# Trace layer of a four-layer kernel: earlier context scan, fuller column tiles, output with tokens on the partitions

## The chip, the cores and the metric

The kernel runs on one core of a Trainium2 chip. The metric is the device time of one execution in microseconds (us). TensorE is PE in the profile, VectorE is DVE, ScalarE is ACT, GpSimd is POOL, SyncE is SP.

## What is computed

`x` is 32 batches of 256 tokens by 256 channels. Four layers run one after the other, each with a residual: sparse attention, a trace layer, an expert MLP, a last attention. The change touches the second one alone:

```python
ctx = causal_ema(x, tau_ctx)                                  # h[t] = alpha*h[t-1] + x[t]
wg = sigmoid(concat([x, ctx]) @ Wg.T + bg)
gated = x * wg
h1 = gelu(x @ Wn1.T + bn1)
mod = 0.5 + sigmoid(h1 @ Wn2.T + bn2)                         # 32 traces per token
traces = [causal_ema(gated * mod[..., d], tau_raws[d]) for d in range(32)]
temporal = sum_d traces[d] * softmax(blend)[d]
gate = sigmoid(temporal @ Wtemp.T + btemp)
soma = gelu(x @ Wsoma.T + bsoma)
out = (soma * gate) @ Wout.T
out = (out - out.mean(-1)) / sqrt(out.var(-1) + 1e-5) * gamma + beta
x = x + out
```

## The kernel before

All 32 batches of `x` stay in SBUF (`X`), with the channels on the partitions (2 blocks of 128) and the 256 tokens in the free dimension. A layer is one block of five hand-written instruction streams, one for each engine, with semaphores between them; nothing reorders them. In the trace layer (`trace_layer`) every engine goes through the same loop over the batches: `body(0)`, then 15 times two bodies, then `body(31)`. The body of batch n mixes three batches: the inputs and gates of batch n + 1 (`has_a`), the traces of batch n, and the output of batch n - 1 (`has_c`).

**Split products.** A product of two fp32 matrices is made of three fp32r matmuls on high and low parts (`product`, L1267). A high part is an ACT copy to fp32r; a low part is a subtraction, made by POOL for `x` and the context (`low_inputs`, L907 and L909) and by DVE for `temporal` and `mixed` (L1038 and L1042).

**Context.** DVE scans the two channel blocks of the next batch (`context`, L938) at the start of a body; ACT makes the high part, POOL the low part, and PE uses both in `gate_in`.

**Traces.** The tokens are cut into chunks of 8. What reaches a chunk from earlier ones: PE sums gated inputs against decay factors (`states`, L1317; POOL prepares the factors in `decays`, L897), DVE weighs the sums by the blend (`state`, L1011), and PE spreads them over the tokens of a chunk (`spread`, L1328). A spread matmul is 128 rows by 32 columns of the array; its output lands on 32 partitions of `pY`, chosen by `tile_position=(0, 32*j)`. There are four calls of `spread` in a batch, of two matmuls each, with j = 0, 1 or 2, 3. ACT copies the result out (`outer_t`, L1174), PE turns it back to channels (`turn_back`, L1336). Inside a chunk, eight lags are made by PE (`lags`, L1345) into two PSUM buffers and summed by DVE (`lag_sum`, L1020 to L1028). DVE's `total` (L1034) adds both parts to `temporal`.

**Output of batch n - 1.** ACT makes the high part of `temporal` (L1133), DVE the low part (L1038), PE the product with Wtemp (`gate_out`, into `pY`), ACT the tanh (L1187), DVE `mixed` (L1048) and its low part, PE the product with Wout (`output`, channels on the partitions of `pZ`). The mean is already taken out of Wout. For the variance ACT squares `pZ` (L1193), PE multiplies the squares by a matrix of 1/256 (`mean_square`, L1372, plain fp32), which leaves the same variance on all partitions; ACT takes the root (L1198) and then calls a Gelu on one column to have that table loaded again (L1200); DVE takes the reciprocal of 128x256 (L1054) and multiplies (L1057); ACT applies gamma and beta (`scaling`, L1206), POOL adds the result to `X` (`residual`, L903).

**Around a batch's end** PE runs states 3, spread 2, lags 6, spread 3, lags 7, `soma_in` (the product with Wsoma), `turn` (transposes of the gated input of batch n + 1), `turn_back`, lags 0 and 1 and states 0 and 1 of batch n + 1, and then `gate_out(n)`, which begins with this wait:

```python
        def gate_out(n):
            pe.wait_ge(templo_done, n + 1)
```

Of the kernel before, what the change touches and what calls it, by code (L numbers as in the profile page):

```python
# [14 lines left out]
P = 128  # L15
S = 256
# [725 lines left out]
def trace_layer(nc, sem_ctx, ctx, t, X, NB, consts):  # L742
# [17 lines left out]
    def sem(name):  # L760
# [36 lines left out]
    mean_mat = sb("mean_mat", [P, P])  # L797
# [14 lines left out]
    state = [sb(f"state{i}", [P, 2, D]) for i in range(2)]  # L812
# [7 lines left out]
    square = sb("square", [P, C, S])  # L820
    std = sb("std", [P, S])
    rstd = sb("rstd", [P, S])
    normed = sb("normed", [P, C, S])
    scaled = sb("scaled", [P, C, S])
# [19 lines left out]
    out_mm, sq_done, var_mm, std_done, rstd_done, normed_done, scaled_done, x2_done = (  # L844
        sem(n) for n in ("out_mm", "sq", "var_mm", "std", "rstd", "normed", "scaled", "x2"))
# [16 lines left out]
    def loop(eng, body):  # L862

        body(0, 0, True, False)
        if NB > 2:
            with pairs(eng, 1, NB - 1) as n:
                body(n, 1, True, True)
                body(n + 1, 0, True, True)
        body(NB - 1, 1, False, True)
# [13 lines left out]
    def _(pool):  # L883
# [27 lines left out]
        def body(n, par, has_a, has_c):  # L911
# [6 lines left out]
        low_inputs(0, 0)  # L918
        pool.wait_ge(set_done, 1)
        decays(0, 0)  # L920
        loop(pool, body)
# [4 lines left out]
    def _(dve):  # L926
# [16 lines left out]
        link(dve.memset(mean_mat[:], 1.0 / D))  # L943
# [107 lines left out]
        def norm(n):  # L1051
# [3 lines left out]
            dve.wait_ge(rstd_done, n + 1)  # L1055
            at_least(dve, scaled_done, n)
            dve.tensor_tensor(normed[:], pZ[:], rstd[:].unsqueeze(1).to_broadcast([P, C, S]), ALU.mult).then_inc(normed_done, 1)  # L1057

        def body(n, par, has_a, has_c):
            if has_a:  # L1060
# [883 lines left out]
```

## Time and profile before

| | us |
|---|---|
| median of 3 runs (2218.88 to 2220.06) | 2219.59 |
| span of the profiled execution | 2220.5 |
| PE busy | 2051.3 (92% of the span) |
| DVE busy | 1699.0 (77%) |
| ACT busy | 1196.2 (54%) |
| POOL busy | 796.4 (36%) |

The profiled execution comes with its span and with no device time of its own; the span stands 0.9 us above the median of the runs. The second layer takes from about 950 to 1703 us of the span; the chain that ended last goes back only into the fourth layer, since a barrier stands between layers, so this chain tells nothing of the second. Busy times of PE are those of pipelined matmuls and overlap: a matmul that lasts 0.28 us can be followed by the next after 0.12 us. Start-to-start distances are the better measure of what a stretch of PE costs.

### The profile page before, as it was taken

How to read it: one execution, taken by the hardware profiler on the slowest of the kernel's cores; microseconds unless marked ns; L12 is line 12 of the kernel's file. 1: busy time of each engine (PE TensorE's matmuls, PEld its weight loads, DVE VectorE, ACT ScalarE, POOL GpSimd, SP SyncE). 2: the span in 40 equal slices, each digit the busy share in tenths (PEclk: the TensorE clock that was granted, in tenths of full speed). 3: DMA queues.
4: the chain of work that ended last, by engine and by line, in shares of the span. 5: the costliest groups of instructions: out<-in, count | busy, mean ns of one | idle time of the engine just before them, and what ended most of it. 6: DMA issues, size and time to landing. Idle time of an engine off the chain costs nothing. (4 is left out here: it accounts for less than half of the span.)

```text
span 2220.5 us, 42789 instructions
## 1 busy us (share of the span) xinstructions
PE 2051.3 (92%) x14158; PEld 1652.1 (74%) x14158; DVE 1699.0 (77%) x2530; ACT 1196.2 (54%) x2428; POOL 796.4 (36%) x589
## 2 busy tenths in 40 slices
PE   3899999999999999759999999999995999999998
PEld 2566666666666666447777777777774999999997
DVE  6788888888888888577878888887875566666664
ACT  2466565666665666435555555555554555555553
POOL 4645444444455554033333333333340111111111
PEclk8999999999999999879999999999997999999998
DMA  3444444444444444100000000000001222222221
GB/s 92 106 106 107 107 110 110 108 109 108 105 105 106 108 109 104 24 25 1 0 0 0 0 0 0 0 0 0 0 0 59 78 79 70 85 69 80 85 66 60
DMA packets 121171, 137.47 MB, mean 62 GB/s; under 512 B 24240, under 2 KB 89776, under 8 KB 121136
## 3 DMA queue, kind: packets, MB, share of 16 engines
q1 hardware_dynamic: 118576, 128.64, 22.9%
q0 software_dynamic: 2560, 8.39, 1.0%
q8 instruction: 19, 0.31, 0.1%
q14 instruction: 16, 0.13, 0.0%
HBM read 48.35 MB, written 8.39 MB: 26 GB/s over the span
## 5 line engine op out<-in xcount | busy, mean ns | idle before, releaser
L366 DVE TENSOR_REDUCE a_neg_max<-a_s 128x2 f32<-128x512 f32 x512 | 329.1, 683 | 123.4 <-PE a_s L613 121.8
L487 ACT ACTIVATE a_e<-a_t 128x512 f32<-128x512 f32 x512 | 281.2, 610 | 228.4 <-PE a_t L626 228.4
L375 DVE SCALAR_TENSOR_TENSOR a_e<-a_e,a_w_t 128x1024 f32<-128x1024 f32 x256 | 373.6, 1469 | 4.1 <-ACT a_e L487 4.1
L613 PE MATMUL a_s<-a_k_st,a_q_st 96*128 96x256 f32 x1024 | 275.4, 380 | 0.0
L613 PEld LDWEIGHTS a_s<-a_k_st,a_q_st 96*128 96x128 f32 x1024 | 203.5, 199 | 13.7
L610 PE MATMUL a_s<-a_add_m,ident_bf 128*128 128x512 bf16 x512 | 201.8, 394 | 7.9 <-POOL a_add_m L254 5.8
L1695 ACT ACTIVATE c_hid<-c_pH,c_b 128x256 f32<-128x256 f32 x256 | 107.4, 471 | 186.3 <-PE c_pH L1758 185.9
L897 POOL TENSOR_TENSOR b_decayed<-b_table,b_mod_t 128x1024 f32<-128x1024 f32 x64 | 118.6, 1872 | 210.3 <-ACT b_mod_t L1163 203.0
L1317 PE MATMUL b_pS<-b_gated_t,b_decayed 128*128 128x256 f32 x768 | 189.5, 390 | 0.7
L626 PE MATMUL a_t<-a_q_st,a_k_st 97*128 97x512 f32 x512 | 177.1, 426 | 2.6 <-DMA a_q_st<-a_max_row 2.0
L642 PE MATMUL a_v<-a_e,a_v_pad 128*32 128x256 f32 x2048 | 163.6, 392 | 4.5 <-DVE a_e L375 2.1
L1317 PEld LDWEIGHTS b_pS<-b_gated_t,b_decayed 128*128 128x128 f32 x768 | 139.3, 191 | 35.1 <-issue 19.7
L1758 PE MATMUL c_pH<-c_x_hi,c_w_hi 128*128 128x256 f32 x512 | 149.8, 293 | 15.4 <-DVE c_w_lo L1660 15.2
L281 POOL TENSOR_TENSOR x_all<-a_delta,x_all 128x512 f32 (+1 forms) x32 | 46.6, 1456 | 323.1 <-ACT a_delta L468 323.1
L1573 POOL TENSOR_TENSOR c_w2b_lo<-c_we,c_w2b_hi 128x512 fp32r<-128x512 f32 x32 | 54.9, 1714 | 277.5 <-ACT c_w2b_hi L1688 277.5
L1758 PE MATMUL c_pH<-c_x_hi,c_w_lo 128*128 128x256 f32 x512 | 145.5, 284 | 0.0
L1758 PE MATMUL c_pH<-c_x_lo,c_w_hi 128*128 128x256 f32 x512 | 145.0, 283 | 0.0
L1028 DVE TENSOR_TENSOR b_inner<-b_inner,b_prod 128x448 f32<-128x448 f32 (+6 forms) x224 | 122.5, 547 | 23.8
L1599 DVE CAST c_hid_hi<-c_hid 128x512 fp32r<-128x512 f32 x128 | 54.5, 425 | 111.2 <-PE c_pO L1772 91.8
L610 PEld LDWEIGHTS a_s<-a_add_m,ident_bf 128*128 128x128 bf16 x512 | 49.6, 97 | 116.3 <-issue 69.8
L1011 DVE TENSOR_TENSOR b_state<-b_pS,b_w_rep 128x512 f32<-128x512 f32 x128 | 85.2, 685 | 56.3 <-PE b_pS L1317 56.3
L1345 PE MATMUL b_pL<-b_mod_st,b_w_st 96*128 96x256 f32 x512 | 116.1, 319 | 2.3 <-DVE b_mod_st L1005 1.0
(261 smaller groups left out, 5720.4 us busy)
## 6 DMA issues: line engine op xcount, KB each, us to landing
a_q_st<-a_q_hi SPq DMA_DIRECT2D x256, 128.0 KB, 2.4
a_k_st<-a_k_hi SPq DMA_DIRECT2D x256, 64.0 KB, 2.0
a_q_st<-a_q_lo SPq DMA_DIRECT2D x128, 128.0 KB, 2.4
a_xs<-in_xT SPq DMA_DIRECT2D x32, 256.0 KB, 2.8
a_k_st<-a_k_lo SPq DMA_DIRECT2D x128, 64.0 KB, 2.1
x_all<-in_xT SPq DMA_DIRECT2D x32, 256.0 KB, 2.8
c_we<-in_we SPq DMA_DIRECT2D x32, 256.0 KB, 2.7
c_key_t<-in_keyT SPq DMA_DIRECT2D x32, 256.0 KB, 3.2
```

Source lines behind the costliest of these rows:

```text
L366: dve.tensor_reduce(neg_max[:, qc, head:head + 2], ps_s[b][:], AX.X, ALU.max, negate=True).then_inc(red_done, 1)
L375: dve.scalar_tensor_tensor(out=buf[:], in0=buf[:], scalar=BIG, in1=w_t[par][:, kc].unsqueeze(1).to_broadcast([P, 4, S]), op0=ALU.min, op1= ...
L487: act.activation(e[g % E_BUFS][:, 2 * b:2 * b + 2], ps_t[b][:], ACT.Exp).then_inc(exp_done, 1)
L610: pe.matmul(ps_s[b][:], ident_bf[:], add_m[par][:, qc].unsqueeze(1).to_broadcast([P, 2, S]), start=True, stop=False)
L613: ins = pe.matmul(ps_s[b][:, r], q_st[par][0:96, slot, qc * P:qc * P + P], k_st[par][0:96, slot // 2], start=False, stop=(r == 1))
L626: pe.matmul(ps_t[b][:], k_st[par][0:97, pair, kc * P:kc * P + P], q_st[par][0:97, 2 * pair:2 * pair + 2], start=True, stop=True).then_inc( ...
L642: ins = pe.matmul(ps_v[half][32 * j:32 * j + 32, quad // 2], v_pad[par][:, kc, 4 * quad + j], e[g % E_BUFS][:, j], start=(g % 4 == 0), sto ...
L897: ins = pool.tensor_tensor(decayed[par][:, lo:lo + cnt], table[:, lo:lo + cnt], mod_t[:, k].unsqueeze(1).to_broadcast([P, cnt, TRACES]), A ...
L1028: dve.tensor_tensor(y, y, pr, ALU.add).then_inc(inner_done, 1)
L1317: ins = pe.matmul(pS[q % 2][:, i], decayed[par][:, lo:lo + 4].rearrange("p a d -> p (a d)"), gated_t[par][:, k], start=(k == 0), stop=(k = ...
L1345: ins = pe.matmul(pL[lag % 2][:, c], w_st[0:3 * TRACES, lag, c * P:c * P + P], mod_st[par][:], start=True, stop=True)
L1758: ins = pe.matmul(pH[r][:, i], w[:, k, m * P:m * P + P], x[par][:, k], start=(w is w1_hi and x is x_hi and k == 0), stop=(x is x_lo and k ...
```

## The change

Bodies of the loop now exist in the forms first, second, 14 times two, last but one, last, since the context runs two batches ahead.

- **Context.** `context(n + 2)` runs in the middle of body n on DVE (after `modulation`), `context(1)` before the loop. DVE's `lag_sum(n, 0)` comes before `low_temporal(n - 1)`, and each other lag sum moves up by one place. ACT's `high_context(n + 2)` stands after `scaling(n - 1)`, ahead of `turned`. POOL's `low_context(n + 2)` is the last of its body, behind `residual(n - 1)`.
- **Spread.** Four `state` buffers in place of two; `spread(n, h)` is called twice with four matmuls, j = 0 to 3, and waits for the second state of its half.
- **Output.** `product(pZ[:, m], mixed_p, wout_p, ...)`: the operands are exchanged, so that tokens lie on the partitions. ACT's `deviation` squares each block of 128x256 with `accum_out` into one column, takes the root of 128x2; DVE's `norm` is a reciprocal of 128x2; ACT's `normalized` multiplies by it. PE turns the result back (`turn_normed`, four transposes into `pB`, after lags 7), and ACT's `scaling` reads `pB`. The matmul with 1/256, and DVE's multiplication, are gone.

```diff
-        def low_inputs(n, par):
+        def low_x(n, par):
             pool.wait_ge(xhi_done, n + 1)
...
+        def low_context(n):
             pool.wait_ge(chi_done, n + 1)
...
         def body(n, par, has_a, has_c, has_x):
             if has_a:
-                low_inputs(n + 1, 1 - par)
+                low_x(n + 1, 1 - par)
+            if has_a:
                 decays(n + 1, 1 - par)
             if has_c:
                 residual(n - 1)
+            if has_x:
+                low_context(n + 2)
...
+        def deviation(n):
             act.wait_ge(out_mm, n + 1)
+            for m in range(C):
+                act.activation(square[:], pZ[:, m], ACT.Square, accum_out=var[:, m:m + 1]).then_inc(sq_done, 1)
+                act.wait_ge(sq_done, C * n + m + 1)
             at_least(act, rstd_done, n)
-            act.activation(std[:], pB[:, 0], ACT.Sqrt, bias=eps[:]).then_inc(std_done, 1)
+            act.activation(std[:], var[:], ACT.Sqrt, bias=eps[:], scale=1.0 / D).then_inc(std_done, 1)
...
+        def normalized(n):
+            act.wait_ge(rstd_done, n + 1)
+            at_least(act, back_done, n)
+            for m in range(C):
+                ins = act.activation(normed[:, m], pZ[:, m], ACT.Copy, scale=rstd[:, m:m + 1])
+            ins.then_inc(normed_done, 1)
...
+        def spread(n, h):
+
+            pe.wait_ge(sw_done, 4 * n + 2 * h + 2)
...
+            for j in range(4):
+                ins = pe.matmul(pY[32 * j:32 * j + 32, h], spread_w[:], state[2 * h + j // 2][:, j % 2],
                                 start=True, stop=True, tile_position=(0, 32 * j))
...
+        def turn_normed(n):
...
+            pe.wait_ge(normed_done, n + 1)
+            for m in range(C):
+                for c in range(C):
+                    ins = pe.transpose(pB[:, c, m * P:m * P + P], normed[:, m, c * P:c * P + P], ident[:])
+            ins.then_inc(back_done, 1)
```

Two places show how the instructions move. The first is PE in a loop body, from states 3 to `soma_in` (`b_pS` is states, `b_pL` lags, `b_spread_w` the spread). Before:

```order
L1317 MATMUL b_pS<-b_gated_t,b_decayed 128x256 x4
L1323 REGISTER_ALU
L1328 MATMUL b_pY<-b_state,b_spread_w 32x256 x2
L1343 REGISTER_ALU
L1345 MATMUL b_pL<-b_mod_st,b_w_st 128x256 x2
L1323 REGISTER_ALU
L1328 MATMUL b_pY<-b_state,b_spread_w 32x256 x2
L1343 REGISTER_ALU
L1345 MATMUL b_pL<-b_mod_st,b_w_st 128x256 x2
L1267 MATMUL b_pZ<-b_x_hi,b_wsoma_hi 128x256
```

After:

```order
L1329 MATMUL b_pS<-b_gated_t,b_decayed 128x256 x4
L1354 REGISTER_ALU
L1356 MATMUL b_pL<-b_mod_st,b_w_st 128x256 x2
L1335 REGISTER_ALU
L1339 MATMUL b_pY<-b_state,b_spread_w 32x256 x4
L1354 REGISTER_ALU
L1356 MATMUL b_pL<-b_mod_st,b_w_st 128x256 x2
L1384 MATMUL b_pB<-ident,b_wtemp 128x128 x4
L1279 MATMUL b_pZ<-b_x_hi,b_wsoma_hi 128x256
```

Of two spreads with two matmuls, one with four is left, lags 6 comes before it, and the transposes of `normed` (which now shares the storage of `b_wtemp`) stand between lags 7 and `soma_in`.

The second place is the end of a body and the start of the next. POOL before (`b_decayed` is `decays`, `x_all<-b_scaled` the residual):

```order
L897 TENSOR_TENSOR b_decayed<-b_table,b_mod_t 128x512
L903 ISA
L903 TENSOR_TENSOR x_all<-b_scaled,x_all 128x2x256
L906 REGISTER_ALU
L907 ISA
L907 TENSOR_TENSOR b_x_lo<-x_all,b_x_hi 128x512
L909 TENSOR_TENSOR b_ctx_lo<-b_ctx_e,b_ctx_hi 128x512
```

POOL after (`b_wtemp` and `b_wsoma` are now also the storage of `normed` and `scaled`):

```order
L898 TENSOR_TENSOR b_decayed<-b_table,b_mod_t 128x512
L904 ISA
L904 TENSOR_TENSOR x_all<-b_wsoma,x_all 128x2x256
L911 REGISTER_ALU
L912 TENSOR_TENSOR b_ctx_lo<-b_ctx_e,b_ctx_hi 128x512
L908 ISA
L908 TENSOR_TENSOR b_x_lo<-x_all,b_x_hi 128x512
```

The context's low part has moved from behind the low part of `x` to between it and the residual.

DVE at the same place, before:

```order
L1034 TENSOR_TENSOR b_temporal<-b_inner,b_pY 128x512
L938 ISA
L938 SCALAR_TENSOR_TENSOR b_ctx_e<-b_alpha_c,x_all 128x256
L938 ISA
L938 SCALAR_TENSOR_TENSOR b_ctx_e<-b_alpha_c,x_all 128x256
L1038 TENSOR_TENSOR b_temp_lo<-b_temporal,b_temp_hi 128x512
L1008 ISA
L1010 REGISTER_ALU
L1011 TENSOR_TENSOR b_state<-b_pS,b_w_rep 128x512
```

DVE after:

```order
L1042 TENSOR_TENSOR b_temporal<-b_inner,b_pY 128x512
L1023 ISA
L1028 TENSOR_TENSOR b_inner<-b_gated,b_pL 128x512
L1046 TENSOR_TENSOR b_temp_lo<-b_temporal,b_temp_hi 128x512
L1016 ISA
L1018 REGISTER_ALU
L1019 TENSOR_TENSOR b_state<-b_pS,b_w_rep 128x512
L1016 REGISTER_ALU
L1019 TENSOR_TENSOR b_state<-b_pS,b_w_rep 128x512
```

The two scans between `total` and the low part of `temporal` are gone from here, and the first lag product has taken their place.

## Rows read from the trace of the kernel before

**Rows 1.** Stages, second layer (window: us, busy PE PEld DVE ACT POOL, PEclk, DMA)
```profile
1000.00:1600.00 600.00, 565.98 (x3779) 469.61 (x3780) 485.69 (x836) 321.82 (x620) 226.85 (x135) 1.00 0.00 0
```

**Rows 2.** Timeline of PE, one batch: start, duration, line, tiles, count [idle before]
```profile
1200.54 0.39 PE L1267 MATMUL b_pY<-b_temp_hi,b_wtemp_hi 128*128 128x256 f32 x1 [1.23 <-DVE b_temp_lo L1038]
...
1207.75 0.63 PE L1328 MATMUL b_pY<-b_state,b_spread_w 128*32 128x256 f32 x4
1208.31 1.99 PE L1317 MATMUL b_pS<-b_gated_t,b_decayed 128*128 128x256 f32 x8
1210.14 1.03 PE L1372 MATMUL b_pB<-b_square,b_mean_mat 128*128 128x256 f32 x4
1210.82 0.59 PE L1345 MATMUL b_pL<-b_mod_st,b_w_st 96*128 96x256 f32 x2
...
1214.74 0.62 PE L1328 MATMUL b_pY<-b_state,b_spread_w 128*32 128x256 f32 x4
...
1215.72 0.63 PE L1328 MATMUL b_pY<-b_state,b_spread_w 128*32 128x256 f32 x4
...
1216.62 0.28 PE L1267 MATMUL b_pZ<-b_x_hi,b_wsoma_hi 128*128 128x256 f32 x1
...
1218.05 0.60 PE L1302 MATMUL b_pA<-ident,b_gated 128*128 128x128 f32 x4
1218.49 0.60 PE L1336 MATMUL b_pY<-ident,b_outer_t 128*128 128x128 f32 x4
...
1219.52 1.99 PE L1317 MATMUL b_pS<-b_gated_t,b_decayed 128*128 128x256 f32 x8
1222.84 0.39 PE L1267 MATMUL b_pY<-b_temp_hi,b_wtemp_hi 128*128 128x256 f32 x1 [1.33 <-DVE b_temp_lo L1038]
```

**Rows 3.** Timeline of DVE, the same batch
```profile
1214.84 0.69 DVE L1011 TENSOR_TENSOR b_state<-b_pS,b_w_rep 128x512 f32<-128x512 f32 x1
...
1217.20 0.98 DVE L1028 TENSOR_TENSOR b_inner<-b_inner,b_prod 128x128 f32<-128x128 f32 x1
...
1219.29 0.69 DVE L1034 TENSOR_TENSOR b_temporal<-b_inner,b_pY 128x512 f32<-128x512 f32 x1 [0.52 <-PE b_pY L1336]
1219.91 2.30 DVE L938 TENSOR_TENSOR_SCAN b_ctx_e<-b_alpha_c,x_all 128x256 f32<-128x256 f32 x2
1222.13 0.66 DVE L1038 TENSOR_TENSOR b_temp_lo<-b_temporal,b_temp_hi 128x512 fp32r<-128x512 f32 x1
```

**Rows 4.** Timeline of PE in the first layer: four column tiles at once
```profile
405.32 0.64 PE L642 MATMUL a_v<-a_e,a_v_pad 128*32 128x256 f32 x8
```

**Rows 5.** Timeline of POOL, the same batch
```profile
1216.22 1.81 POOL L903 TENSOR_TENSOR x_all<-b_scaled,x_all 128x512 f32 x1 [3.98 <-ACT b_scaled L1206]
1220.03 1.63 POOL L907 TENSOR_TENSOR b_x_lo<-x_all,b_x_hi 128x512 fp32r<-128x512 f32 x1 [2.00 <-ACT b_x_hi L1123]
1223.03 1.31 POOL L909 TENSOR_TENSOR b_ctx_lo<-b_ctx_e,b_ctx_hi 128x512 fp32r<-128x512 f32 x1 [1.37 <-ACT b_ctx_hi L1128]
```

**Rows 6.** Timeline of ACT, the same batch
```profile
1211.20 0.48 ACT L1198 ACTIVATE b_std<-b_pB,b_eps 128x256 f32<-128x256 f32 x1 [1.05 <-PE b_pB L1372]
...
1213.10 0.82 ACT L1144 ACTIVATE b_th_g<-b_pA,b_bg 128x256 f32<-128x256 f32 x2
1214.94 1.09 ACT L1206 ACTIVATE b_scaled<-b_normed,b_beta,b_gamma 128x256 f32<-128x256 f32 x2 [1.02 <-DVE b_normed L1057]
...
1218.69 0.60 ACT L1169 ACTIVATE b_gated_t<-b_pA 128x512 f32<-128x512 f32 x1 [1.69 <-PE b_pA L1302]
...
1220.01 0.63 ACT L1133 ACTIVATE b_temp_hi<-b_temporal 128x512 fp32r<-128x512 f32 x1 [0.18 <-DVE b_temporal L1034]
```

**Rows 7.** Groups of instructions by line, fourth layer, ACT (count | busy us, mean ns)
```profile
L1703 ACT ACTIVATION_READ_ACCUMULATOR c_prob<-c_pS,c_neg_max 128x1 f32 x62 | 12.2, 196 | 0.0
```

**Rows 8.** Busy time by stage, last body of the second layer (columns as in rows 1)
```profile
1668.00:1672.50 4.50, 2.68 (x17) 1.62 (x16) 3.61 (x7) 1.47 (x3) 0.00 (x0) 1.00 0.00 0
1673.00:1675.50 2.50, 2.50 (x14) 1.89 (x12) 1.26 (x3) 0.47 (x1) 0.00 (x0) 0.50 0.01 3
```

More of the change, by code:

```diff
@@ L811, in trace_layer @@
     decayed = [sb(f"decayed{i}", [P, TABLE, TRACES]) for i in range(2)]
-    state = [sb(f"state{i}", [P, 2, D]) for i in range(2)]
+    state = [sb(f"state{i}", [P, 2, D]) for i in range(4)]
     inner = sb("inner", [P, C, S])
@@ L819, in trace_layer @@
     mixed = sb("mixed", [P, C, S])
[L820 to L824, printed above, removed]
+    square = sb("square", [P, D])
+    var = sb("var", [P, C])
+    std = sb("std", [P, C])
+    rstd = sb("rstd", [P, C])
+    normed = wtemp
+    scaled = wsoma
     pA = ps("pA", [P, C, S])
@@ L862, in loop @@
     def loop(eng, body):
[L864 to L869, printed above, removed]
+        body(0, 0, True, False, True)
+        body(1, 1, True, True, True)
+        with pairs(eng, 2, NB - 2) as n:
+            body(n, 0, True, True, True)
+            body(n + 1, 1, True, True, True)
+        body(NB - 2, 0, True, True, False)
+        body(NB - 1, 1, False, True, False)
     @block.sync
@@ L1054, in norm, with body @@
             dve.reciprocal(rstd[:], std[:]).then_inc(rstd_done, 1)
[L1055 to L1060, printed above, removed]
-                context(n + 1)
+        def body(n, par, has_a, has_c, has_x):
+            lag_sum(n, par, 0)
             if has_c:
@@ L1086, in body @@
             total(n)
+        context(1)
         gating(0, 0)
@@ L1231, in body @@
             if has_c:
+                normalized(n - 1)
+            spread_out(n)
+            if has_c:
                 scaling(n - 1)
-            spread_out(n)
+            if has_x:
+                high_context(n + 2)
             if has_a:
@@ L1248, in _ @@
         high_mixed(NB - 1)
[L1249 removed]
         deviation(NB - 1)
+        normalized(NB - 1)
         scaling(NB - 1)
@@ L1319, in states @@
             ins.then_inc(st_done, 1)
-        def spread(n, q):
-            pe.wait_ge(sw_done, 4 * n + q + 1)
-            if q == 0:
+        def spread(n, h):
+            pe.wait_ge(sw_done, 4 * n + 2 * h + 2)
+            if h == 0:
                 at_least(pe, tho_done, n)
-            for i in range(2):
-                j = (2 * q + i) % 4
-                ins = pe.matmul(pY[32 * j:32 * j + 32, q // 2], spread_w[:], state[q % 2][:, i],
+            for j in range(4):
+                ins = pe.matmul(pY[32 * j:32 * j + 32, h], spread_w[:], state[2 * h + j // 2][:, j % 2],
                                 start=True, stop=True, tile_position=(0, 32 * j))
@@ L1363, in output, with body @@
             for m in range(C):
-                ins = product(pZ[:, m], wout_p, mixed_p, [(k, k) for k in range(C)], m)
+                ins = product(pZ[:, m], mixed_p, wout_p, [(k, k) for k in range(C)], m)
             ins.then_inc(out_mm, 1)
-        def mean_square(n):
+        def turn_normed(n):
             pe.wait_ge(tht_done, NB if isinstance(n, int) and n + 3 > NB else n + 3)
-            pe.wait_ge(sq_done, n + 1)
-            for k in range(C):
-                ins = pe.matmul(pB[:, 0], mean_mat[:], square[:, k], start=(k == 0), stop=(k == C - 1))
-            ins.then_inc(var_mm, 1)
-        def body(n, par, has_a, has_c):
+            pe.wait_ge(normed_done, n + 1)
[3 more added lines that the diff above has]
+            ins.then_inc(back_done, 1)
+        def body(n, par, has_a, has_c, has_x):
             lags(n, par, 0)
@@ L1390, in body @@
                 modulate_rows(n + 1)
+            spread(n, 0)
             if has_c:
```

62 lines of the change are left out of this document (26 added, 36 removed).

## Prediction

> **What bounds the kernel now.** The layers are separated by barriers, so I read the second layer's own stages first and the chain that ended last not at all: it ends in the fourth layer. In 600 us of steady second layer PE is busy for 566 us, DVE for 486, ACT for 322, POOL for 227, and PE's granted clock is 1.00, its upper level of 2.4 GHz [rows 1]. So PE is the bound, nearly full, and a batch can only become shorter by less PE work or less PE waiting.
>
> Then PE's timeline of one batch. `gate_out` starts at 1200.54 and again at 1222.84, so the period is 22.30 us [rows 2]. PE has one real wait in it: the states that start at 1219.52 need 1.83 us (1208.31 to 1210.14 for the same eight records), so PE is free at 1221.35 and starts `gate_out` at 1222.84. That wait is 1.49 us [rows 2].
>
> Then DVE, to see why. `total` starts at 1219.29, ACT has the high part of `temporal` ready at 1220.01 + 0.63 = 1220.64, but DVE stands in two scans from 1219.91 and makes the low part only at 1222.13 [rows 3, 6].
>
> Last, who slows whom. The residual on POOL takes 1.81 us and its neighbour of the same 128x512 takes 1.31 [rows 5]. A DVE sum of 128x128 which reads SBUF twice takes 0.98 us, and it ends at 1218.18, just after the residual's end at 1218.03 [rows 3, 5]. POOL's low part of x runs from 1220.03 to 1221.66, and the second scan ends at 1222.21, 0.55 us after it [rows 3, 5]. So an operation of DVE with two SBUF inputs and a POOL operation do not run beside each other: the later one waits for the whole of the earlier one, and then DVE needs 0.55 us more.
>
> **The change part by part, on PE.** I compare one period with 22.30.
>
> *Scans moved.* The wait of 1.49 us goes, as far as the low part of `temporal` comes in time (below). In mid-batch DVE has room: it loses the big reciprocal and the multiplication, and was busy 486 of 600 us.
>
> *Spreads.* A spread of two matmuls costs 0.56 us (1207.75 to 1208.31) [rows 2]. Four matmuls of the same 128x32 by 256 on four column tiles last 0.64 us in the first layer, where two last 0.63 here [rows 2, 4]: four cost what two do. The bounds are 0.56 and 1.12 us for four; I take 0.56, since that row is the same shape. The first half saves 0.56. The second saves less. Before, spread 3 started 0.98 us after spread 2 (1214.74 to 1215.72) [rows 2], with lags 6 in between and state 3 ready meanwhile. Now the only spread follows lags 6 and must wait for state 3, whose weighing starts 0.10 us after states 3 and lasts 0.69 [rows 3]: about 0.83 us with the handoff. Gain 0.15, and PE has a new wait of some 0.4 us there; lags 7 and everything of the batch's end stand behind it.
>
> *Variance.* The matmul with 1/256 goes: 0.68 us (1210.14 to 1210.82) [rows 2]. Four transposes come: 0.44 us as `turn` (1218.05 to 1218.49), at most the 0.68 that it replaces [rows 2]; I take 0.60 for the change of kind of matmul behind it. The exchange of operands in `output` changes neither count nor shape: nothing. `gate_out` to `output` stays as long as before, since the chain over tanh, `mixed` and its low part crosses a lag sum on DVE as before, only the next smaller one.
>
> Sum on PE, if the low part is in time: 22.30 - 1.49 - 0.56 - 0.15 - 0.68 + 0.60 = 20.02 us.
>
> **The batch's end after the change.** Let T be the start of the new transposes. `soma_in` takes 1.43 us (1216.62 to 1218.05) [rows 2], so `turn` starts at T + 2.03, PE is free for `gate_out` 0.44 + 1.03 + 1.83 = 3.30 later (1218.05, 1218.49, 1219.52 [rows 2]), at T + 5.33. DVE's `total` starts 1.24 us after `turn`, ACT's high part 0.72 after that [rows 2, 3, 6], and it ends 0.63 later: the low part can start at T + 4.65 (a lag product of 0.6 us fits in front of it). It takes 0.66 and ends at T + 5.31: just in time.
>
> Now POOL. Transposes to their reader on ACT: 0.64 us (1218.05 to 1218.69) [rows 2, 6]. `scaling` from PSUM: 0.82 as the two tanh [rows 6]; handoff to POOL 0.19 (1214.94 + 1.09 to 1216.22) [rows 5, 6]. The residual starts at T + 1.65 and takes 1.31, as nothing of DVE with two SBUF inputs runs then; the context's low part, whose input ACT has made by then, takes 1.31 more, to T + 4.27. The low part of x for the next batch follows at once (before the change it started 1.98 us after `turn`, 1218.05 to 1220.03 [rows 2, 5], so its input is there by T + 4.0) and holds POOL from T + 4.3 to T + 5.6. DVE's low part of `temporal` arrives at T + 4.65, 0.35 us too late. It then ends at T + 5.6 + 0.55 = T + 6.15, and `gate_out` starts 0.05 later (1222.13 + 0.66 to 1222.84 [rows 2, 3]) at T + 6.2 in place of T + 5.33. Price: 0.84 us a batch, so the period is 20.86 and the gain 1.44 us.
>
> The Trainium skill (SBUF — State Buffer, "SBUF: two separate sides") says the same: a DVE operation with two SBUF inputs and a GpSimd operation that reads SBUF share a port pair, and whichever starts first "gets the pair for the whole instruction; the other fully blocks". This rule speaks against the change, which puts three POOL operations in a row right where DVE's critical subtraction falls; without it the sum would be the 20.02 above. The trace agrees, with the 0.98 and the 1.81 us named above.
>
> **Outside the steady batches.** Thirty periods get the full gain. Ahead of the loop DVE now runs two scans (2.3 us) before `gated(0)`, and body 0 loses them: about nothing. At the end the three DVE and PE steps of the last norm give way to steps on ACT and transposes: between -2 and +2. The sum: 30 x 1.44 = 43 us. The profiled span is 0.9 us above the median, so I subtract from the median: 2219.6 - 43 = **2176 us**.
>
> **Rivals.**
>
> A, the forecast: the low part of x gets ahead of the low part of `temporal`. For it: 0.35 us of lead. Chance 0.56, own range 2166 to 2186.
>
> B: the lead is not there. Handoffs in a row on POOL of 0.1 us more each, or transposes of 0.44, would turn the order. Then DVE's subtraction runs first, POOL waits where nobody needs it, and the period is 20.0 to 20.1: 30 x 2.25 = 67 us, 2152 us. Chance 0.30.
>
> C: the new transposes wait for their input, or four tiles don't overlap. ACT's chain is longer by two read-outs of the accumulator (0.20 each [rows 7]) and by cutting one square in two, and shorter by the 1.05 us that the root waited for PE [rows 6]; so the gate's tanh starts some 0.6 us earlier than its 12.56 us after `gate_out` (1213.10), and the normalized blocks (2 x 0.82 later) are there about 13.6 us after `gate_out`, where PE comes at 14.7 (`turn` came at 17.51 before, 0.79 less after the sum above, and T lies 2.03 ahead of it). The slack is 1.1 us. If ACT is 1.9 us later than this, 0.8 us a batch is lost: 2176 + 24 = 2200 us. Spreads that cost 1.12 give 1.1 us back a batch, 2209 us, which the row of the first layer speaks against. Chance 0.09 together.
>
> D, slower than before: the clock. In the last body, with PE busy 2.68 of 4.50 us, the granted clock is 1.00 and then 0.50 (1.2 GHz) in the following stretch of full work [rows 8]. The steady loop now has two waits, 0.4 and 0.84 us, in place of one of 1.49. If they brought such a fall in each batch, work of 1.44 us at half the speed takes as much again: from there on the gain is gone, and with 2 us of work the kernel is slower by 30 x 0.56 = 17 us, 2236 us. Against it: the loop took its 1.49 us at a granted clock of 1.00 [rows 1], and the new waits are 6 us apart and smaller together. Chance 0.03. That nothing comes of it at all, the gain lost in one place and the rest in another, has 0.02.
>
> **Numbers.** Forecast 2176. From 2149 (B with a batch 0.1 us shorter) to 2188, below C's times; about 0.1 lies above, the rest of B below. A measurement of this kernel tells a change of about 0.2% (4.4 us) from none. A, B and C are all faster: 0.95. Within 0.2%: 0.02. Slower: 0.03.
>
> **What would show it.** In the changed profile: `gate_out` to `gate_out` 20.9 us; a wait of about 0.4 us before the second spread, released by the state; spreads of eight records at 0.56 to 0.65 us; the low part of `temporal` lasting 1.4 us or more in place of 0.66 and ending 0.55 us after POOL's low part of x; a wait of 0.8 us before `gate_out`. A `gate_out` that follows the states at once, and a low part of 0.66 us, would be B. A wait ahead of the transposes released by ACT would be C, a granted clock under 1.00 in the loop D.

## The result and the profile after

| | before | changed |
|---|---|---|
| median, us | 2219.82 (2218.88 to 2220.47) | 2169.43 (2167.51 to 2170.3) |
| span of the profiled execution, us | 2220.5 | 2167.9 |
| a batch of the steady second layer, us | 22.29 | 20.64 |

The ratio is 0.9772, with a 95% interval of 0.9758 to 0.9786. The change makes the kernel faster by 50 us, or 2.3%. The forecast was 2176 us with a range of 2149 to 2188, by case A.

The steady second layer of the changed kernel, in the stretch and columns of [rows 1]:

```profile
1000.00:1600.00 600.00, 559.35 (x4075) 485.49 (x4074) 454.40 (x873) 368.70 (x815) 223.81 (x145) 1.00 0.00 0
```

PE is busy for 559 of 600 us, 7 less than before, since it now waits in two places. DVE lost 31 us and ACT gained 47. The granted clock is 1.00 as before. More batches fit: 4075 matmul records against 3779.

PE's timeline of one batch of the changed kernel, which answers to [rows 2]:

```profile
1203.86 0.39 PE L1279 MATMUL b_pY<-b_temp_hi,b_wtemp_hi 128*128 128x256 f32 x1 [0.80 <-DVE b_temp_lo L1046]
...
1208.52 0.64 PE L1339 MATMUL b_pY<-b_state,b_spread_w 128*32 128x256 f32 x8
1209.09 0.39 PE L1279 MATMUL b_pZ<-b_wout_hi,b_mixed_hi 128*128 128x256 f32 x1
...
1210.99 1.97 PE L1329 MATMUL b_pS<-b_gated_t,b_decayed 128*128 128x256 f32 x8
1212.61 0.58 PE L1356 MATMUL b_pL<-b_mod_st,b_w_st 96*128 96x256 f32 x2
...
1214.71 1.89 PE L1329 MATMUL b_pS<-b_gated_t,b_decayed 128*128 128x256 f32 x8
1216.25 0.58 PE L1356 MATMUL b_pL<-b_mod_st,b_w_st 96*128 96x256 f32 x2
1217.38 0.64 PE L1339 MATMUL b_pY<-b_state,b_spread_w 128*32 128x256 f32 x8 [0.56 <-DVE b_state L1019]
1217.95 0.50 PE L1356 MATMUL b_pL<-b_mod_st,b_w_st 96*128 96x256 f32 x2
1218.29 0.60 PE L1384 MATMUL b_pB<-ident,b_wtemp 128*128 128x128 f32 x4
1218.65 0.36 PE L1279 MATMUL b_pZ<-b_x_hi,b_wsoma_hi 128*128 128x256 f32 x1
...
1220.16 0.60 PE L1314 MATMUL b_pA<-ident,b_gated 128*128 128x128 f32 x4
...
1221.71 1.99 PE L1329 MATMUL b_pS<-b_gated_t,b_decayed 128*128 128x256 f32 x8
1224.50 0.39 PE L1279 MATMUL b_pY<-b_temp_hi,b_wtemp_hi 128*128 128x256 f32 x1 [0.80 <-DVE b_temp_lo L1046]
```

`gate_out` to `gate_out` is 20.64 us in this batch. The prediction's T is 1218.29. Both spreads are of eight records and last 0.57 us from start to start of what follows. The two waits stand where the prediction put them: the profile lists 0.56 us ahead of the second spread, for the state, and 0.80 ahead of `gate_out`, for the low part of `temporal`. A listed wait is shorter than one taken from start to start, as the prediction takes them, since it begins where the profile lets the last matmul end: the prediction's 1.49 us before the change is listed as 1.33 [rows 2].

What DVE and POOL did at the batch's end, in answer to [rows 3] and [rows 5], DVE first:

```profile
1210.92 1.27 DVE L946 TENSOR_TENSOR_SCAN b_ctx_e<-b_alpha_c,x_all 128x256 f32<-128x256 f32 x2
...
1216.64 0.69 DVE L1019 TENSOR_TENSOR b_state<-b_pS,b_w_rep 128x512 f32<-128x512 f32 x1 [0.57 <-PE b_pS L1329]
...
1222.18 0.69 DVE L1028 TENSOR_TENSOR b_inner<-b_gated,b_pL 128x512 f32<-128x512 f32 x1
1222.85 1.59 DVE L1046 TENSOR_TENSOR b_temp_lo<-b_temporal,b_temp_hi 128x512 fp32r<-128x512 f32 x1
```

Then POOL:

```profile
1220.14 1.28 POOL L904 TENSOR_TENSOR x_all<-b_wsoma,x_all 128x512 f32 x1 [4.34 <-ACT b_wsoma L1217]
1221.37 1.29 POOL L912 TENSOR_TENSOR b_ctx_lo<-b_ctx_e,b_ctx_hi 128x512 fp32r<-128x512 f32 x1
1222.63 1.26 POOL L908 TENSOR_TENSOR b_x_lo<-x_all,b_x_hi 128x512 fp32r<-128x512 f32 x1
```

The low part of x starts 0.22 us before the low part of `temporal` and ends at 1223.89. DVE's subtraction, begun at 1222.85, ends at 1224.44: 0.55 us after POOL's end, and 1.59 us long where it was 0.66. The two scans, now in mid-batch, take 1.27 us together where they took 2.30.

The scaling no longer starts after a root that waited for PE; it starts behind the new transposes (ACT's timeline, in answer to [rows 6]):

```profile
1218.93 1.02 ACT L1217 ACTIVATE b_wsoma<-b_pB,b_beta,b_gamma 128x256 f32<-128x256 f32 x2 [0.25 <-PE b_pB L1384]
...
1222.19 0.63 ACT L1139 ACTIVATE b_temp_hi<-b_temporal 128x512 fp32r<-128x512 f32 x1 [0.17 <-DVE b_temporal L1042]
```

### The profile page after: what moved, and what is told of

Same layout as the page of the kernel before. It is cut to its first block and busy times, and to the rows that moved or that the text cites. A ratio compares the mean times of both kernels' runs of the same rounds, so it can differ in the third digit from the quotient of the medians.

```text
span 2167.9 us, 42832 instructions
## 1 busy us (share of the span) xinstructions
PE 1993.4 (92%) x14158; PEld 1630.0 (75%) x14158; DVE 1620.8 (75%) x2498; ACT 1220.5 (56%) x2588; POOL 776.8 (36%) x589
## 3 DMA queue, kind: packets, MB, share of 16 engines
q1 hardware_dynamic: 118576, 128.64, 23.1%
## 5 line engine op out<-in xcount | busy, mean ns | idle before, releaser
L898 POOL TENSOR_TENSOR b_decayed<-b_table,b_mod_t 128x1024 f32<-128x1024 f32 x64 | 127.1, 2007 | 270.6 <-ACT b_mod_t L1169 263.3
L1329 PEld LDWEIGHTS b_pS<-b_gated_t,b_decayed 128*128 128x128 f32 x768 | 139.6, 191 | 22.3 <-issue 6.7
L1036 DVE TENSOR_TENSOR b_inner<-b_inner,b_prod 128x448 f32<-128x448 f32 (+6 forms) x224 | 113.2, 505 | 22.7
L1031 DVE TENSOR_TENSOR b_prod<-b_gated,b_pL 128x448 f32<-128x448 f32 (+6 forms) x224 | 94.2, 421 | 36.5 <-PE b_pL L1356 36.4
L440 ACT ACTIVATE a_q_full<-a_bank,a_bq_s,par_mask 128x256 f32<-128x256 f32 x128 | 65.8, 574 | 89.7 <-PE a_bank L575 75.4
```

What stands on the lines that cost most here:

```text
L898: ins = pool.tensor_tensor(decayed[par][:, lo:lo + cnt], table[:, lo:lo + cnt], mod_t[:, k].unsqueeze(1).to_broadcast([P, cnt, TRACES]), A ...
L1036: dve.tensor_tensor(y, y, pr, ALU.add).then_inc(inner_done, 1)
L1329: ins = pe.matmul(pS[q % 2][:, i], decayed[par][:, lo:lo + 4].rearrange("p a d -> p (a d)"), gated_t[par][:, k], start=(k == 0), stop=(k = ...
```

## The experiments

Every ratio below is against the kernel before, timed beside the kernel in question. The theory under test is case A with the sum behind it; the rivals are that other parts carry the gain. "Period" is the time from one batch's high part of `temporal` to the next, for odd and even batches where they differ.

### Is it POOL that holds the low part?

The first kernel puts POOL's low part of x behind DVE's low part of `temporal`.

```diff
             if has_a:
+                at_least(pool, templo_done, n)
                 low_x(n + 1, 1 - par)
```

> The changed kernel, in which POOL's low part of x waits until DVE has made the low part of temporal. Theory (the two operations exclude each other and POOL is ahead by 0.22 us): DVE's low part takes 0.66 to 0.69 us in place of 1.6, the wait before gate_out goes, the period falls from 20.69 by 0.8 us to about 19.9, the time from 2169 to about 2145. Rival (gate_out is late for another reason, such as ACT's high part or the lag product ahead of it): the low part is not shorter or the wait stays, and the time is 2169 or a little more, since the wait puts POOL's work later.

Measured: 2144.28 us, ratio 0.9658 (0.9641 to 0.9674), period 19.77 and 19.83. Timeline of this kernel, DVE and then POOL:

```profile
1212.90 0.69 DVE L1047 TENSOR_TENSOR b_temp_lo<-b_temporal,b_temp_hi 128x512 fp32r<-128x512 f32 x1
```

```profile
1213.86 1.29 POOL L908 TENSOR_TENSOR b_x_lo<-x_all,b_x_hi 128x512 fp32r<-128x512 f32 x1 [1.17 <-DVE b_temp_lo L1047]
```

The low part takes 0.69 us again, and PE's wait ahead of `gate_out` is gone from its list of waits (23.3 us in 29 times in the changed kernel, between 1000 and 1600 us). The period falls by 0.84 us, which is the price that the prediction gave. It shows the price, but a wait on a semaphore also orders more than the two operations. So the next two leave all waits as they are and only shift POOL, by small memsets behind the context's low part. They write storage that nobody reads.

```diff
+    idle = sb("idle", [P, 16])
...
             if has_x:
                 low_context(n + 2)
+                for i in range(4):
+                    pool.memset(idle[:, 4 * i:4 * i + 4], 0.0)
```

> The changed kernel with four idle memsets of 128x4 on POOL between the context's low part and the low part of x; no wait is added. Theory (whoever starts first has the port for its whole operation, and POOL leads by 0.22 us): if the four together take more than 0.22 us the order turns over, DVE's low part takes 0.66 to 0.69 us, and the time is about 2145 us although POOL has more to do. Rival (the two share bandwidth, or DVE's low part is slow by itself): it stays near 1.6 us or ends later by the length of the memsets, and the time is 2169 to 2180 us.

Measured: 2172.59 us, ratio 0.9785 (0.9769 to 0.9802), period 20.68 and 20.86. The order did not turn over. POOL and DVE of this kernel:

```profile
1222.59 0.19 POOL L925 MEMSET b_idle<- 128x4 f32 x4
1222.75 1.26 POOL L909 TENSOR_TENSOR b_x_lo<-x_all,b_x_hi 128x512 fp32r<-128x512 f32 x1
```

```profile
1222.86 1.70 DVE L1049 TENSOR_TENSOR b_temp_lo<-b_temporal,b_temp_hi 128x512 fp32r<-128x512 f32 x1
```

The four memsets took only 0.2 us. POOL's lead of 0.22 us shrank to 0.11, and DVE's subtraction became longer by the 0.11, since it still ends 0.55 after POOL. The batch became 0.13 us longer by it (20.64 to 20.77 on average); the times, 2169.43 and 2172.59 us, are too near each other to tell the two kernels apart by their ratios. Twelve memsets in the same place are the test of the turn-over:

> As e2, but with twelve memsets in place of four. Four took 0.20 us together and moved POOL's low part of x by 0.12 us; its lead over DVE's low part fell from 0.22 to 0.11 us and the low part of temporal ended 0.1 us later. Twelve take about 0.6 us. Theory (first come, whole operation): POOL now comes 0.3 us late, DVE's low part takes 0.69 us, the period falls to 19.8 us and the time to about 2145 us. Rival (every delay of POOL is passed on): each further 0.1 us costs 3 us, so about 2182 us.

Measured: 2143.92 us, ratio 0.9651 (0.9635 to 0.9667), period 19.65 and 19.75.

```profile
1213.96 0.69 DVE L1049 TENSOR_TENSOR b_temp_lo<-b_temporal,b_temp_hi 128x512 fp32r<-128x512 f32 x1
```

```profile
1213.70 0.44 POOL L925 MEMSET b_idle<- 128x4 f32 x12
1214.38 1.44 POOL L909 TENSOR_TENSOR b_x_lo<-x_all,b_x_hi 128x512 fp32r<-128x512 f32 x1 [0.24 <-issue]
```

Twelve instructions of no use on POOL, 0.68 us with their issue, make the kernel 26 us faster than the change alone. No wait, no engine's order and no matmul is different from the kernel with four. The low part of x now meets an operation already running and is the one that is stretched (1.44), where nobody needs it. This is the test that A needed: which of the two operations comes first decides 0.84 us a batch by the first of these kernels and 1.07 by the last two (20.77 to 19.70, on average). The rule of the Trainium skill that the prediction cites, that whichever starts first has the shared ports for its whole instruction (SBUF — State Buffer, "SBUF: two separate sides"), agrees with both kernels with memsets: with four, DVE comes second and takes 1.70 us; with twelve, POOL does and takes 1.44.

The third way is to give POOL the low part of x first and the context's after it. The kernel before had them in that order.

```diff
             if has_a:
                 low_x(n + 1, 1 - par)
-            if has_a:
+                low_context(n + 1)
                 decays(n + 1, 1 - par)
             if has_c:
                 residual(n - 1)
-            if has_x:
-                low_context(n + 2)
...
-        low_context(1)
```

> The changed kernel with POOL's low part of x ahead of the context's low part again; nothing else moved. Theory (first come, whole operation): the low part of x starts when its high part is there, 3.85 us after the transposes of the normalized block, and holds POOL to 5.1; DVE's low part, which wants to start at 4.56, ends at 5.65 in place of 6.16. Period 20.64 to 20.15 us, time about 2154 us. Rival (any order is as good as that with the wait of e1, since POOL is done sooner): 2145 us; or no effect: 2169.

Measured: 2159.82 us (2154 expected), ratio 0.9713 (0.9696 to 0.9731), period 20.16 and 20.28. POOL and DVE of this kernel:

```profile
1220.73 1.28 POOL L908 TENSOR_TENSOR b_x_lo<-x_all,b_x_hi 128x512 fp32r<-128x512 f32 x1 [0.81 <-ACT b_x_hi L1126]
1221.96 1.75 POOL L912 TENSOR_TENSOR b_ctx_lo<-b_ctx_e,b_ctx_hi 128x512 fp32r<-128x512 f32 x1
```

```profile
1221.36 1.20 DVE L1043 TENSOR_TENSOR b_temp_lo<-b_temporal,b_temp_hi 128x512 fp32r<-128x512 f32 x1
```

The low part of `temporal` comes in the middle of the low part of x. It still ends 0.55 after it (1222.01 and 1222.56), but POOL's end lies earlier, so it takes 1.20 us and not 1.59. The context's low part, the next on POOL, was begun at 1221.96 and takes 1.75, to 1223.71: DVE, which was already waiting, went between two operations of POOL. So this order gives about half of what the other two kernels give (0.42 us of the batch).

### What each part is worth

The spread alone is undone: four spreads of two matmuls, in their old places.

```diff
-            for j in range(4):
-                ins = pe.matmul(pY[32 * j:32 * j + 32, h], spread_w[:], state[2 * h + j // 2][:, j % 2],
+            for i in range(2):
+                j = (2 * q + i) % 4
+                ins = pe.matmul(pY[32 * j:32 * j + 32, q // 2], spread_w[:], state[q][:, i],
...
             states(n, par, 3)
+            spread(n, 2)
             lags(n, par, 6)
-            spread(n, 1)
+            spread(n, 3)
```

> The changed kernel with four spreads of two matmuls again, each in its old place; context and output stay changed. Theory (PE is the bound up to each wait, four tiles cost what two do): one spread of 0.56 us more ahead of states 2, and the second spread starts 0.98 us after the matmuls of state 3 were followed by a spread, about 0.13 us later than now: 0.69 us a batch, time about 2190 us. Rival (the batch is bound by the chain over DVE and ACT, and PE's extra work only fills its waits): 2169 to 2175 us.

Measured: 2193.94 us (2190 expected), ratio 0.9877 (0.9861 to 0.9894), period 21.35 and 21.50. PE's waits between 1000 and 1600 us (us in total, times, longest) have one row left:

```profile
PE b_pY L1279 <- DVE b_temp_lo L1046: 23.3, 28, 0.9
```

The wait for the state is gone with the second spread's new place, and 0.78 us a batch is lost. The prediction's terms for the spreads were 0.56 + 0.15 = 0.71.

The context is put back to the start of a body, on DVE, ACT and POOL:

```diff
         def body(n, par, has_a, has_c, has_x):
+            if has_a:
+                context(n + 1)
             lag_sum(n, par, 0)
             if has_c:
                 low_temporal(n - 1)
...
-            if has_x:
-                context(n + 2)
             lag_sum(n, par, 4)
...
```

> The changed kernel with the context scanned at the start of the body for the next batch again (DVE, ACT and POOL in the old order there); spreads and output stay changed. Theory (scans, lag product and low part in a row on DVE, with POOL's low part of x between the two scans): the low part ends 1.15 us later than in the changed kernel, period 21.8, time about 2204 us. Rival (the lock has eaten what moving the context gave, since POOL's low context now stands in the same place): within 6 us of 2169.

Measured: 2225.0 us (2216.81 to 2226.47), ratio 1.0007 (0.9995 to 1.0018): no faster than the kernel before, and 21 us over the 2204 expected. Batches last either 21.6 to 21.8 us, as the theory has it, or 23.1 to 23.3, some 18 of 30. Here are a long batch's wait, and busy time and granted clock (the last but two columns) in four stretches, three behind that wait and one behind the next, of 1.83 us, which ended at 1223.82; last the row of the whole stretch.

```profile
1200.62 0.39 PE L1275 MATMUL b_pY<-b_temp_hi,b_wtemp_hi 128*128 128x256 f32 x1 [1.84 <-DVE b_temp_lo L1043]
```

```profile
1200.60:1203.50 2.90, 2.88 (x18) 2.88 (x19) 2.33 (x5) 1.09 (x3) 1.12 (x1) 0.74 0.00 0
1203.60:1206.50 2.90, 2.90 (x18) 2.85 (x18) 2.31 (x5) 1.03 (x2) 0.00 (x0) 0.69 0.00 0
1206.80:1209.00 2.20, 2.20 (x23) 1.78 (x22) 1.57 (x5) 0.38 (x1) 0.00 (x0) 1.00 0.00 0
1223.80:1226.00 2.20, 2.19 (x18) 2.19 (x19) 2.17 (x4) 0.62 (x3) 1.12 (x1) 1.00 0.00 0
...
1000.00:1600.00 600.00, 536.32 (x3729) 468.21 (x3728) 408.84 (x799) 340.57 (x748) 216.29 (x132) 0.95 0.00 0
```

Behind the wait of 1.84 us PE is fully busy, at a granted clock of 0.74 and then 0.69: part of the time at 1.2 GHz, and the rest at 2.4. Behind the next wait it is 1.00. So not each such wait brings the clock down, but 18 of 30 batches show it. This kernel also has the wait of 0.56 us for the state in each batch. That is the mechanism of case D, in a kernel that the prediction did not ask about. To show it as the cause, a further kernel fills the wait: the same, with twelve matmuls (Wsoma with x, into `pA`, used by nobody) ahead of `gate_out`.

```diff
             states(n, par, 1)
             if has_c:
+                for m in range(C):
+                    product(pA[:, m], wsoma_p, x_p[par], [(k, k) for k in range(C)], m)
                 gate_out(n - 1)
```

> e3, with twelve matmuls of no use (the product with Wsoma once more, into the PSUM tile that gate_in overwrites later) ahead of gate_out, where PE waited 1.84 us. Theory (the long batches of e3, 23.1 to 23.3 us against 21.6 to 21.8, come from the clock that falls after this wait): PE now works for 1.4 us of the wait, the granted clock is 1.00 throughout, all batches take 21.7 us, and the time falls from 2225 to about 2200 us although PE does more. Rival (the clock falls for another reason, or the long batches have another cause): 2225 us or more.

Measured: 2199.92 us, ratio 0.9896 (0.9879 to 0.9913), all periods 21.61 or 21.75.

```profile
1000.00:1600.00 600.00, 572.36 (x4214) 505.65 (x4213) 422.77 (x832) 354.94 (x778) 225.01 (x138) 1.00 0.00 0
```

More work and 25 us less time; of the wait, 0.41 us is left in the list. All batches are now as long as the short ones of the kernel without the filling, so the wait itself cost what the sum said (2199.92 us against 2204), and the clock after it the rest. So within this change the move of the context is worth 30 us by its wait (2199.92 against 2169.43), and another 25 us by the clock, which that wait brings down.

The variance is put back as it was, with everything else as changed:

```diff
-            for m in range(C):
-                act.activation(square[:], pZ[:, m], ACT.Square, accum_out=var[:, m:m + 1]).then_inc(sq_done, 1)
...
+            act.activation(square[:], pZ[:], ACT.Square).then_inc(sq_done, 1)
...
             dve.reciprocal(rstd[:], std[:]).then_inc(rstd_done, 1)
...
+            dve.tensor_tensor(normed[:], pZ[:], rstd[:].unsqueeze(1).to_broadcast([P, C, S]), ALU.mult).then_inc(normed_done, 1)
...
             states(n, par, 2)
+            if has_c:
+                mean_square(n - 1)
             lags(n, par, 4)
...
-            if has_c:
-                turn_normed(n - 1)
             soma_in(n, par)
```

> The changed kernel with the output's channels on the partitions and the variance by a matmul again; context and spreads stay changed. Theory: PE has 0.3 us a batch more to do, POOL's residual is earlier, which brings DVE's low part forward by 0.5 us, but the reciprocal of 128x256 and the multiplication (2.4 us) now stand ahead of state 3 on DVE and the second spread waits for state 3: 1.7 us later. Together 1.4 us a batch, about 2212 us. Rival (DVE has room for the reciprocal, so only PE's 0.3 us and POOL's gain count): 2160 to 2178 us.

Measured: 2268.56 us, ratio 1.0218 (1.0201 to 1.0235), where 2212 was expected. The shortest batches are 22.3 us, the others 24.1 and 25.4. PE, and DVE ahead of it:

```profile
1204.71 0.64 PE L1333 MATMUL b_pY<-b_state,b_spread_w 128*32 128x256 f32 x8 [2.58 <-DVE b_state L1020]
```

```profile
1200.86 1.73 DVE L1063 RECIPROCAL b_rstd<-b_std 128x256 f32<-128x256 f32 x1
1202.62 0.69 DVE L1066 TENSOR_TENSOR b_wtemp<-b_pZ,b_rstd 128x512 f32<-128x512 f32 x1
...
1203.97 0.68 DVE L1020 TENSOR_TENSOR b_state<-b_pS,b_w_rep 128x512 f32<-128x512 f32 x1
```

The reciprocal of 128x256 and the multiplication stand ahead of the weighing of state 3 on DVE, and with the scans also in mid-batch they come late. The single spread behind lags 6 needs that state: PE waits 2.58 us for it. In the changed kernel the reciprocal is 0.15 us. The expectation had this queue on DVE, and the shortest batches agree with it: 22.3 us, 1.67 more than in the changed kernel, where 1.4 was expected. What it left out is the clock, which is 1.00 in such a batch and falls in others. PE behind the next of these waits, and the busy time and granted clock of the stretch:

```profile
1227.51 1.08 PE L1333 MATMUL b_pY<-b_state,b_spread_w 128*32 128x256 f32 x8 [2.68 <-DVE b_state L1020]
```

```profile
1227.50:1230.50 3.00, 2.99 (x17) 2.18 (x18) 2.27 (x5) 1.11 (x2) 2.33 (x2) 0.50 0.00 0
```

The clock is at its lower level, 1.2 GHz, and `soma_in` takes 2.56 us there where it takes 1.44 in a short batch. It takes over 2 us in 15 of the 25 batches between 1000 and 1600 us, and the batches of that stretch last 23.93 us on average. By the distance of this from 22.3, about half of the 99 us that this kernel lost against the change is the clock (an estimate: 30 x 1.6 = 49 us). No run has this kernel with its wait filled, so that share is read from the batches and not shown by an experiment.

The last of these makes one part alone: the kernel before, with only the context moved.

```diff
         def body(n, par, has_a, has_c, has_x):
-            if has_a:
-                context(n + 1)
             if has_c:
                 low_temporal(n - 1)
...
                 modulation(n + 1, 1 - par)
+            if has_x:
+                context(n + 2)
             states(n, 2)
```

> The kernel before with the context moved alone (scans in mid-batch on DVE behind modulation, its high part ahead of turned on ACT, its low part behind the residual on POOL); spreads, output and the order of the lag sums as before. Theory: POOL's low part of x now runs from 1.98 to 3.25 us after turn, since it only waits for its high part; DVE's low part wants to start at 2.7 and ends at 3.8 in place of 4.74. Period 22.3 to 21.4 us, time about 2192 us. Rival (the wait of 1.49 us goes whole): 21.0 us or less, 2178 us; or scans in mid-batch delay state 2 and state 3 on DVE and eat the gain: 2210 to 2225 us.

Measured: 2268.25 us, ratio 1.0204 (1.0186 to 1.0222), periods 23.3 to 24.9. That is neither the theory's 2192 nor a rival's time, though one rival named the mechanism: scans in mid-batch that delay states 2 and 3. The target itself was hit: PE's wait ahead of `gate_out` fell to 0.38 us:

```profile
1216.40 0.38 PE L1276 MATMUL b_pY<-b_temp_hi,b_wtemp_hi 128*128 128x256 f32 x1 [0.38 <-DVE b_temp_lo L1045]
```

But in mid-batch DVE's scans ran into POOL's `decays` (DVE, then POOL):

```profile
1199.84 4.38 DVE L945 TENSOR_TENSOR_SCAN b_ctx_e<-b_alpha_c,x_all 128x256 f32<-128x256 f32 x2
```

```profile
1199.58 4.09 POOL L898 TENSOR_TENSOR b_decayed<-b_table,b_mod_t 128x1024 f32<-128x1024 f32 x2 [8.58 <-ACT b_mod_t L1171]
```

The two scans, 1.27 us together in the changed kernel, took 4.38 beside `decays`. The old reciprocal and multiplication follow them, and then the state: PE waited for it 47.7 us in 25 times (longest 2.0) between 1000 and 1600 us. Behind some of these waits the clock fell here too; this is the stretch behind the one of 1.87 us that ended at 1208.71:

```profile
1208.70:1210.30 1.60, 1.59 (x7) 0.78 (x8) 1.38 (x4) 0.98 (x3) 0.93 (x1) 0.52 0.00 0
```

`soma_in` takes over 2 us in 10 of the 25 batches of the stretch, and 1.43 or 1.44 in the others. So the parts don't add up. Context alone costs 47 us (2268.25 against 2221.65); context and spread without the variance cost 47 (2268.56 against 2221.2); all three gain 50. By these rows, what the small reciprocal buys is room on DVE for the scans and for state 3, and with it a wait of PE short enough to leave the clock at 1.00.

### What is left

With the low part of x held back (the first experiment), PE still waits 0.56 us for the state. Two further kernels start from there. In one, lags 7 goes ahead of the second spread:

```diff
             lags(n, par, 6)
-            spread(n, 1)
             lags(n, par, 7)
+            spread(n, 1)
```

> e1 (POOL's low part of x waits for DVE's low part) and PE's lags 7 put ahead of the second spread, where PE waits 0.56 us for state 3. Theory (the wait is real and the end of the batch hangs on the spread): the matmuls of lags 7 (0.24 us) disappear in the wait, period 19.8 to 19.55 us, about 2137 us against 2144. Rival (DVE's lag sum 7 or the turned output is what counts): 2144 us.

Measured: 2136.03 us, ratio 0.9615 (0.9599 to 0.9631), period 19.48 and 19.55. The wait became 0.32 us each.

In the other, the context half of `gate_in` moves behind states 3, and ACT makes `normalized` ahead of the gate's tanh:

```diff
             lags(n, par, 4)
-            if has_a:
-                gate_in(n + 1, 1 - par, 1)
             lags(n, par, 5)
             states(n, par, 3)
+            if has_a:
+                gate_in(n + 1, 1 - par, 1)
             lags(n, par, 6)
...
-            if has_a:
-                input_gate(n + 1)
             if has_c:
                 normalized(n - 1)
+            if has_a:
+                input_gate(n + 1)
```

> e1, with the second half of gate_in (1.44 us of PE) moved from between lags 4 and 5 to behind states 3, and ACT's normalized block ahead of the gate's tanh. Theory: state 3 is summed 1.4 us earlier and weighed while gate_in runs, so the wait of 0.56 us before the second spread goes nearly wholly; the tanh comes 0.9 us later but has room. Period 19.8 to 19.3 us, about 2129 us. Rival (the tanh, then the gated input and its transposes come too late and make a new wait before turn): 2144 us or more.

Measured: 2125.95 us (2125.24 to 2126.96), ratio 0.9574 (0.9558 to 0.959), period 19.14 and 19.20. PE's timeline and the stretch of the steady layer:

```profile
1214.22 0.64 PE L1340 MATMUL b_pY<-b_state,b_spread_w 128*32 128x256 f32 x8
```

```profile
1000.00:1600.00 600.00, 589.53 (x4304) 514.54 (x4302) 445.50 (x921) 395.86 (x865) 229.58 (x150) 0.99 0.00 0
```

Twelve matmuls, 1.4 us of work that depends on nothing late, cover the state's way through DVE. The profile lists no wait in the steady batches any more, and PE is busy for 589.5 of 600 us; the 0.99 comes with the layer's last batches, whose waits of up to 3 us fall into this stretch. About a quarter of a microsecond is still lost unlisted ahead of `gate_out`:

```profile
1207.50 1.99 PE L1330 MATMUL b_pS<-b_gated_t,b_decayed 128*128 128x256 f32 x8
1209.39 0.39 PE L1280 MATMUL b_pY<-b_temp_hi,b_wtemp_hi 128*128 128x256 f32 x1
```

It starts 1.89 us after the states. In the kernel with the filled wait the next product started 1.64 us after them (1210.85 to 1212.49), with nothing to wait for. Here the low part of `temporal` ends at 1209.34, 0.05 us ahead of `gate_out`, so it still sets the time, as in the kernel of the first experiment (1.89 us too). This is the best kernel of the study: 95 us (4.3%) under the kernel before and 43 us under the change.

## Why the prediction was right, step by step

**The bound.** PE bounded the kernel, and the end of the batch decided. The kernels here follow PE's waits and, in three of them, the clock behind the waits.

**Spreads.** Four matmuls of 128x32 on four column tiles take 0.57 us against 0.56 for two: the lower bound, as taken. The second spread waits for the state, which is ready 2.67 us after states 3 began; by the prediction's terms it was 1.83 + 0.83 = 2.66. From start to start the wait is 0.70 us and not some 0.4, only because lags 6 began 0.28 earlier (below).

**Variance: the term that was mis-sized.** I put the matmul with 1/256 at 0.68 us, the distance to what followed it. What the change gave back is 0.89. Before, plain float32 matmuls stood behind the states and began 1.83 us after their start. Now lags 4 stands there, and lags 6 behind states 3 in the same way, with fp32r operands: 1.62 us (1210.99 to 1212.61) and 1.54 us (1214.71 to 1216.25). The 0.21 us at lags 4 shortens the batch; the 0.28 at lags 6 goes into the wait for the state. From `gate_out` to T the prediction had 14.7 us (17.51 - 0.79 - 2.03 = 14.69); it is 14.43 (1203.86 to 1218.29), 0.26 less. Of this 0.21 is the variance term. Another 0.08 is the first spread, whose removal gave 0.64 us and not 0.56 (`gate_out` to states 2 takes 7.13 us, where it took 7.77), and 0.03 was lost at the second.

**Transposes.** Taken at 0.60, measured 0.36 (1218.29 to 1218.65), with 0.08 of it given back in `soma_in` (1.51 against 1.43). It changed nothing, because the end of the batch is set by POOL. The prediction had said that transposes of 0.44 us would turn the order to B. They were as short as that in effect, and the order stayed: the step from T to their reader on ACT was still 0.64 us, and DVE's operation came only 0.09 us earlier after T.

**The batch's end.** Forecast from T, measured: residual T + 1.65, T + 1.85; low part of x T + 4.3, T + 4.34; low part of `temporal` wanted at T + 4.65, begun T + 4.56; its end T + 6.15, T + 6.15; `gate_out` T + 6.2, T + 6.21. The residual came 0.20 later than forecast, but POOL's three operations then followed closer than 1.31 each. The lead was 0.22 us, not 0.35, and the choice between A and B was narrow, as a chance of 0.30 for B said: four memsets, which moved POOL's operation by about 0.1 us, left A, and twelve made it B. That `gate_out` hit the forecast to 0.01 us is in part luck, since errors of up to 0.2 us on the way to it cancelled.

**The price.** By the prediction's own times it is 6.2 - 5.33 = 0.87 us, not 0.84; the slip is worth 1 us in 2176. PE itself would have been free some 0.2 us before T + 5.33, since that time takes 1.83 us for the states and an fp32r product can follow after 1.64. Yet the time was right for B: in the first experiment the low part, undisturbed, let `gate_out` start at T + 5.31.

**The sizes.** Period 20.64, not 20.86; 30 x 1.65 = 50 us, as measured (50.4). B, made by experiment, has 19.80 us a batch, against 20.02 in the sum: the same 0.22 less. Its 2144.28 us would have been below the range, whose lower end of 2149 allowed B only 0.1 us.

**C.** ACT came in time. The transposes had 1.1 us of slack: `normed` was ready at 1217.16, T is 1218.29.

**D.** In the changed kernel the granted clock stayed at 1.00. But it was near: with the context back, one listed wait grew from 1.23 to 1.33 us in the kernel before to 1.84, the clock fell and took 1.5 us of the batch with it. The mechanism of D is real here. Where it begins, no run shows; in the steady batches it was not seen behind listed waits of up to 1.33 us, and was seen behind some of those of 1.84 us and more.

**Not seen.** The prediction costed DVE's mid-batch by its busy share ("in mid-batch DVE has room"). That held for the three parts together, and only for them. Moved alone, the scans collide with `decays`, and the old reciprocal delays state 3. A busy share of 486 in 600 says nothing of an operation that has to be there at one instant.

## What to carry to other kernels

Where a DVE operation with two SBUF inputs is on the path, look at which POOL operation starts in the microsecond before it: who is first decides, and here 0.7 us of nothing on POOL was worth over 1% of the kernel. A change made of several moves should be tested both one part undone and one part alone: here one part alone, and two of the three together, each cost 2%. When a wait of PE grows beyond what the kernel has shown at full clock, its price is not the wait alone: read the granted clock behind it.

## What the runs showed of the hardware

- A listed wait of PE of 1.84 us in each batch of 21.7 us, with one of 0.56 us besides, brought the granted clock down to 0.74 and 0.69 in the two stretches of nearly 3 us behind it, and some 18 of 30 batches were 1.5 us longer for it. Filling most of the wait with useless matmuls restored 1.00 and made the kernel 25 us faster. In two other kernels a wait of 1.87 us had 0.52 behind it, and one of 2.68 us had 0.50. The clock stayed at 1.00 with a wait of 1.23 to 1.33 us in 22.3, and with two of 0.56 and 0.80 in 20.6.
- DVE's blocked subtraction of 128x512 ended 0.55 us after POOL's operation in the change, with four memsets and with POOL's other order, wherever it had begun, and so did the second scan of 128x256 in the kernel before. So starting it earlier, once POOL has the ports, gains nothing; only POOL's end counts.
- A scan of 128x256 on DVE, whose one input is a broadcast column, is subject to the same exclusion: two took 1.27 us in the changed kernel, 2.30 beside POOL's low part, 4.38 beside `decays`.
- Matmuls with fp32r operands began 1.54 to 1.64 us after the start of eight records of plain float32 ones, where plain ones began after 1.81 to 1.83. It holds for lags of 96 rows and for products of 128 alike; that the kind of operand is the cause was not tested by itself.
